# Feed-forward products of a two-layer retention kernel: split low-precision pairs replaced by plain fp32

## The reference, cut to what matters

```python
# 1. retention with decay mask, group norm, gate, output product (L0_attn_ref) on X
# 2. the feed-forward block that the change is about (L0_ffn_ref), D_IN = 256, D_HID = 1024
def _tlin(x, w, s): return jnp.einsum('bsi,oi->bso', x, w) * s
h = jax.nn.silu(_tlin(x, w1_w, w1_s)) * _tlin(x, w2_w, w2_s)
h = jax.nn.gelu(_tlin(h, h1_w, h1_s), approximate=False)
h = jax.nn.gelu(_tlin(h, h2_w, h2_s), approximate=False)
return _tlin(h, w3_w, w3_s)
# 3. a recurrence over a state of 32 blocks of 8 x 8, four steps (the batch axis) per position
# 4. a two-product mix with the previous position (L1_ffn_ref)
```

## Time and profile before

| | us |
|---|---|
| median of three runs | 1184.78 (1183.74 to 1186.15) |
| the profiled execution, its own time | 1184.52 |
| its span in the trace | 1182.7 |
| PE busy / DVE busy / ACT busy / POOL busy | 1083.8 / 965.1 / 606.7 / 483.6 |
| mean granted clock of TensorE | 0.968 of 2.4 GHz |

### The profile page before, as it was taken

The page is one execution under the profiler, slowest core; times in us unless marked ns, Lnnn a source line. Parts: engine busy times, 40 slices in busy tenths (PEclk is TensorE's granted clock), DMA queues, the critical chain, the costliest instruction groups (busy, mean ns, idle before and its releaser), DMA issues.

```text
span 1182.7 us, 16467 instructions
## 1 busy us (share of the span) xinstructions
PE 1083.8 (92%) x5761; PEld 837.7 (71%) x5761; DVE 965.1 (82%) x1417; ACT 606.7 (51%) x1039; POOL 483.6 (41%) x379
## 2 busy tenths in 40 slices
PE   6999999999999999999999999999999999984434
PEld 3666666677787777788778778877877887772323
DVE  3688888872045998998899899899989989999883
ACT  1345555554345356555735655573565557344552
POOL 1366677774333234344324433432343343231220
PEclk9999999999999999999999999999999999998657
DMA  6334544753522431332333133233313323310000
GB/s 227 128 138 159 190 174 176 275 189 110 175 90 72 134 97 52 110 111 85 95 101 126 44 115 101 94 91 98 130 40 120 96 82 90 95 48 0 0 18 21
DMA packets 45339, 127.02 MB, mean 107 GB/s; under 512 B 4320, under 2 KB 21472, under 8 KB 43104
## 3 DMA queue, kind: packets, MB, share of 16 engines
q1 hardware_dynamic: 44416, 114.72, 30.3%
q10 hardware_dynamic: 864, 11.54, 2.6%
HBM read 117.86 MB, written 19.92 MB: 117 GB/s over the span
## 4 chain that ended last, share of the span: by engine, by line
DVE 55%; PE 25%; issue 9%; ACT 6%; POOL 2%; DMA 1%; DVEq 0%; ACTq 0%; POOLq 0%; SPq 0%
DVE tmp L2015 7%; PE lower L441 7%; PE lower L1164 6%; DVE tmp L2005 6%; DVE Sq L2007 5%; DVE tmp L2021 4%; DVE delta L2017 4%; PE bank L1164 3%; DVE stats L142 2%; PE lower L541 2%; DVE delta L2019 2%; DVE S L2023 2%; ACT look L646 1%; DVE whole L1967 1%; PE bank L471 1%
## 5 line engine op out<-in xcount | busy, mean ns | idle before, releaser
L1830 POOL TENSOR_TENSOR a_lo<-whole,a_hi 128x512 fp32r<-128x512 f32 x128 | 181.8, 1438 | 268.3 <-ACT a_hi L1467 197.1
L1164 PE MATMUL lower<-b_hi,ring 128*128 128x512 f32 x512 | 193.6, 396 | 1.4 <-ACT a_hi L1467 1.4
L1164 PE MATMUL lower<-b_lo,ring 128*128 128x512 f32 x512 | 190.7, 390 | 1.7 <-POOL b_lo L1830 1.7
L1164 PE MATMUL lower<-a_hi,ring 128*128 128x512 f32 x496 | 186.3, 394 | 1.7 <-issue 1.7
L1164 PE MATMUL lower<-a_lo,ring 128*128 128x512 f32 x496 | 184.2, 390 | 0.2 <-POOL a_lo L1830 0.2
L1830 POOL TENSOR_TENSOR b_lo<-whole,b_hi 128x512 fp32r<-128x512 f32 x64 | 93.9, 1474 | 145.1 <-ACT b_hi L1467 145.1
L1450 ACT ACTIVATE S<-S 128x1024 f32<-128x1024 f32 x56 | 58.6, 1059 | 183.0 <-DVE S L2023 183.0
L1466 ACT ACTIVATE whole<-lower,hs 128x512 f32<-128x512 f32 x126 | 86.2, 684 | 76.8 <-PE lower L1164 71.8
L441 PE MATMUL lower<-wa,xT 128*128 128x512 f32 x240 | 111.2, 608 | 10.9 <-DMA wa<-wa_dram 8.0
L1164 PEld LDWEIGHTS lower<-b_hi,ring 128*128 128x128 f32 x512 | 96.2, 188 | 21.9 <-issue 1.8
L1164 PEld LDWEIGHTS lower<-b_lo,ring 128*128 128x128 f32 x512 | 96.0, 188 | 22.0 <-POOL b_lo L1830 2.3
(11 more groups left out here) (278 smaller groups left out, 2361.5 us busy)
## 6 DMA issues: line engine op xcount, KB each, us to landing
ring<-ffn_copy_dram SPq DMA_DIRECT2D x128, 512.0 KB, 3.6
look<-ffn_dram ACTq DMA_DIRECT2D x6, 1879.0 KB, 7.0
ffn_copy_dram<-ffn_dram SPq DMA_DIRECT2D x8, 1408.0 KB, 9.5
xT<-xT_dram SPq DMA_DIRECT2D x8, 512.0 KB, 8.5
rope<-rope_dram SPq DMA_DIRECT2D x8, 512.0 KB, 8.3
xtok<-x_dram SPq DMA_DIRECT2D x8, 512.0 KB, 4.4
x1in<-x_dram SPq DMA_DIRECT2D x8, 512.0 KB, 4.8
x1res<-x_dram SPq DMA_DIRECT2D x8, 512.0 KB, 3.3
```

Source lines behind the costliest of these rows:

```text
L1164: ins = nc.tensor.matmul(out, a, b, start=(first and n == 0), stop=(last and n == len(pairs) - 1))
L1830: nc.gpsimd.tensor_tensor(lo[:, m, :], t["whole"][:, m % 4, :], hi[:, m, :].bitcast(F32), ALU.subtract).then_inc(lo_done, 1)
```

## The change

The branch, the look at the weights and the copy in DRAM go. All feed-forward products are plain fp32 matmuls: the weight tiles and the moving tiles are of type fp32, and a block is one instruction in the program instead of two. The high and low tiles are gone, so all weights fit in SBUF: w1, w2, w3 as before, and `h1` and `h2` (4 MB each), loaded once in 16 pieces behind waits for the attention tiles whose place they take. The results of a layer alternate between an `inner` and a `middle` tile of six slots; two slots of each go to `pairs0` or `pairs1`, which change sides with the parity of the chunk, so the loop of bodies 3 to 6 becomes two rounds of two bodies. Activations write their tile once. The layout of some attention tiles changes with it. The GpSimd stream of a body has only the roots of the layer norms left.

```diff
-        w1r = sb(narrow, "w1r", [P, KD, HID], F32R)
-        w2r = sb(narrow, "w2r", [P, KD, HID], F32R)
-        w3r = sb(narrow, "w3r", [P, KH, DIM], F32R)
+        w1 = sb(top, "w1", [P, KD, HID])
+        w2 = sb(top, "w2", [P, KD, HID])
+        w3 = sb(top, "w3", [P, KH, DIM])
...
-            def copy_piece(c):
-                cols = bass.ds(c * PIECE, PIECE)
-                sp.dma_start(ffn_s[:, cols], ffn_d[:, cols]).then_inc(copy_in, 16)
...
-            def look_load(c):
-                act.dma_start(look[:], ffn_d[:, bass.ds(c * LOOK_STEP, LOOK)]).then_inc(look_in, 16)
-
-            def add_low_bits(c):
-                act.wait_ge(low_bits, c + 1)
-                nc.scalar.activation(look[:], look[:].bitcast(I32), ACT.Copy,
-                                     accum_out=low_sum[:, bass.ds(c, 1)]).then_inc(low_added, 1)
...
+            def first_side(m, parity):
+
+                return pairs[parity][:, m, :] if m < 2 else inner[:, m - 2, :]
+
+            def second_side(m, parity):
+
+                return middle[:, m, :] if m < KH - 2 else pairs[1 - parity][:, m - (KH - 2), :]
...
+            def schedule(eng, body):
+
+                for i in range(3):
+                    body(i, i % 2, True, i >= 1, i >= 2, i + 1 < CHUNKS)
+                with eng.Fori(3, CHUNKS - 2, 2) as i:
+                    body(i, 1, True, True, True, True)
+                    body(i + 1, 0, True, True, True, True)
+                body(CHUNKS - 1, 1, True, True, True, False)
...
+                    sp.wait_ge(proj_done, CHUNKS * BATCH)
+                    for m in (0, 3, 4):
+                        hidden_load(0, m)
+                    sp.wait_ge(rope_done, CHUNKS * BATCH)
+                    for m in (1, 2):
+                        hidden_load(0, m)
+                    sp.wait_ge(r1_done, (CHUNKS - 2) * 2)
+                    xtok_load(CHUNKS - 1, 1)
                     sp.wait_ge(yT_ps, (CHUNKS - 1) * 2)
+                    for m in (5, 6, 7):
+                        hidden_load(0, m)
+                    store(CHUNKS - 3, 1)
+                    sp.wait_ge(yT_ps, CHUNKS * 2)
+                    sp.wait_ge(gw_done, CHUNKS * 4)
+                    for m in range(KH - 1):
+                        hidden_load(1, m)
                     store(CHUNKS - 2, 0)
...
-                            if narrow_w:
-                                w = (w1r, w2r)[n]
-                                pairs = [(w[:, k, cols], x[:, k, :]) for k in range(KD) for x in (t["x1hi"], t["x1lo"])]
...
+                            ins = product(bank[pair(m, c) + n][:], [((w1, w2)[n][:, k, m * P:m * P + P], wide_a[:, k, :])
+                                                                    for k in range(KD)])
...
-                        ins = product(bank_of(n, c)[:], [(w[:, k, :], x[:, k, :]) for k in range(KH) for x in (hi, lo)])
+                        ins = product(bank_of(n, c)[:], [(w[:, m, k, :], src(k, parity))], first=(k == 0),
+                                      last=(k == KH - 1))
...
-                    act.wait_ge(lo_done, c * SPLITS + KH + n - 3)
-                    nc.scalar.activation(t["whole"][:, m % 4, :], bank_of(n, c)[:], ACT.Gelu, scale=scale).then_inc(act_done, 1)
-                    nc.scalar.activation((t["b_hi"], t["a_hi"])[layer][:, m, :], bank_of(n, c)[:], ACT.Gelu,
-                                         scale=scale).then_inc(hi_done, 1)
+                    nc.scalar.activation((second_side, first_side)[layer](m, parity), bank_of(n, c)[:], ACT.Gelu,
+                                         scale=(hs1, hs2)[layer][:, m:m + 1]).then_inc(act_done, 1)
...
-                pe.wait_ge(flag_done, 1)
+                    pe.wait_ge(turn_done, CHUNKS * BATCH)
+                    pe.wait_ge(v_done, CHUNKS * BATCH)
+                    pe.wait_ge(gate_done, CHUNKS * BATCH)
...
+                    act.wait_ge(r1_done, CHUNKS * 2 - 2)
                     silu(5)
```

More of the change, by code:

```diff
@@ L26 @@
 F32 = mybir.dt.float32
-F32R = mybir.dt.float32r
 I32 = mybir.dt.int32
@@ L136, in build @@
         w123_in = sem(top, "w123_in")
+        hidden_in = [[sem(top, f"hidden_in{n}_{m}") for m in range(KH)] for n in range(2)]
         pow_ready = sem(top, "pow_ready")
@@ L243, in build @@
             v[n] = sb(attention, f"v{n}", [P, BATCH, DIM])
-            xtok[n] = sb(attention, f"xtok{n}", [P, BATCH, DIM])
+            if not n:
+                xtok[n] = sb(attention, f"xtok{n}", [P, BATCH, DIM])
         state = sb(attention, "state", [P, BATCH, GROUPS, P])
@@ L1053, in fin_sums, with sync_program, hidden_load @@
                 return ((t["mv3"], t["mean3"]), (t["mv4"], t["mean4"]), (t["mv2"], t["mean2"]))
[L1055 to L1065, removed]
+            def schedule(eng, body):
[5 more added lines that the diff above has]
+                body(CHUNKS - 1, 1, True, True, True, False)
+            def sync_program(sp, store, xtok_load):
                 def x1_rows(c):
                     return x1_d[bass.ds(c, 1)].rearrange("o p b d -> (o p) b d")
[L1070 to L1075, removed]
+                def hidden_load(n, m):
+                    col = (COL_H1, COL_H2)[n] + m * HID
+                    sp.dma_start((h1, h2)[n][:, m].rearrange("p k n -> p (k n)"),
+                                 ffn_d[:, col:col + HID]).then_inc(hidden_in[n][m], 16)
                 out_view = out_d.rearrange("b (c p) d -> p c b d", p=P)
@@ L1125, in body @@
                                      t["y4"][:]).then_inc(out_done, 16)
-                    if more and narrow_w:
-                        for n in range(RING):
-                            ring_load(i + 1, n, i * 2 * KH + 2 * KH - RING + n + 1)
-                schedule(sp, body, 1 if narrow_w else 0)
+                schedule(sp, body)
                 for g, (c, n) in enumerate(PAIRS_LEFT):
@@ L1231, in down @@
-                def down(c):
-                    if narrow_w:
-                        pe.wait_ge(hi_done, c * SPLITS + 3 * KH)
-                        pe.wait_ge(lo_done, c * SPLITS + 3 * KH - 1)
-                    else:
-                        pe.wait_ge(act_done, c * 2 * KH + 2 * KH)
+                    w = (h1, h2)[layer]
+                    src = (first_side, second_side)[layer]
+                    if isinstance(c, int) and c == 0:
+                        pe.wait_ge(hidden_in[layer][m], 16)
@@ L1281, in mix_in, with body @@
                     by_row(wide_b, wr, 6, dr_ps)
-                def body(i, ffn, scan, mix, more):
+                def body(i, parity, ffn, scan, mix, more):
                     c, d = i - 1, i - 2
-                    started = narrow_w and isinstance(i, int) and i == 0
+                    started = isinstance(i, int) and i == 0
                     if ffn and not started:
@@ L2093, in ffn_out, with body @@
                     ln2.end()
-                def body(i, ffn, has_scan, mix, more):
+                def body(i, parity, ffn, has_scan, mix, more):
                     c, d = i - 1, i - 2
                     if has_scan:
-                        ffn_out(c, (lambda: product(i, 2)) if ffn else None)
-                    if ffn and not (narrow_w and isinstance(i, int) and i == 0):
+                        ffn_out(c, (lambda: product(i, parity, 2)) if ffn else None)
+                    if ffn and not (isinstance(i, int) and i == 0):
                         for m in range(3 if has_scan else 2, KH):
-                            product(i, m)
+                            product(i, parity, m)
                     if mix:
@@ L2114, in body @@
                         mix_result(d)
-                    if more and narrow_w:
-                        x1_low(i + 1)
                     if has_scan:
@@ L2330, in start @@
                     end.norm_stats(last, 1)
-                if narrow_w:
-                    start()
-                    prepare()
-                else:
-                    prepare()
-                    for m in range(2):
-                        product(0, m)
+                start()
+                prepare()
                 schedule(dve, body)
@@ L2419, in _ @@
             def _(dve):
-                end = attention_vector(dve)
-                flag = wide_words(dve)
-                with dve.If(flag < 1):
-                    steps = vector_program(dve, True, end)
-                with dve.Else():
-                    attention_ends(dve, end.body)
-                    assert vector_program(dve, False, end).k == steps.k
+                steps = vector_program(dve, attention_vector(dve))
                 last_mix(dve, steps)
```

419 lines of the change are left out of this document (98 added, 321 removed).

## The result

| | before | after |
|---|---|---|
| median of the runs | 1185.3 us (1183.74 to 1186.15, 4 runs) | 1728.39 us (1727.13 to 1732.06, 4 runs) |
| profiled execution, its span | 1184.52, 1182.7 us | 1728.57, 1726.6 us |
| ratio of the runs, 95% interval | | 1.4589 (1.4562 to 1.4617) |

A forecast was written before the change was run, and what follows sets the result against it. TensorE was taken as the bound, so its added work is paid nearly in full: 1184.5 + 517 + 48.6 - 8.6 - 4.5 - 2.4 = 1734.6, forecast 1735 us, range 1700 to 1790.

The forecast's parts named there:

- The bound: Feed-forward pipeline: TensorE idles only 9.6 of 822 us, so added work is paid nearly in full; period 103.7 to 174.4 us.
- The price of a wide block: `up` and `hidden`, 512 columns: 0.8575 us in plain fp32 against 0.4537 as a split pair; 1280 blocks, +517 us.
- The three checks that the forecast set: Bodies: period near 174 us with PE busy throughout, DVE below 60%; `hidden` blocks starting 0.857 us apart, two records each.
- The price of a narrow block: `down`, 256 columns: 0.43 us in plain fp32 against 0.24 a split pair; 256 blocks, +48.6 us (43 to 50).
- Products, gaps and `down` together: Feed-forward pipeline: +517 us for `up` and `hidden`, +48.6 for `down`, -8.6 of PE's 9.6 us idle time.
- The look and the attention stage: Attention stage: removing ScalarE's six 3.355 us looks at the weights and DVE's masks gives -4.5 us, bounds 0 and -7.9.
- The loads of h1 and h2, the waits added, the longer loop: Weight loads, new waits, two-body loop: 0 us; late pieces 3 us each, 24 at most; loop up to 2 a round.
- Is PE fed: Top of a body, x2 transposes: PE runs 17.2 us of `up` after `down` instead of 9.1; slack grows from 1 to 9.
- The end: After the last `down`: first key norm 3.4 us after row 0's turn instead of 5.8, -2.4 us; remaining 115.4 us stay.
- Two passes: Rival, feed-forward products: an fp32 product costs one record's step, 0.429 us instead of 0.4537, giving 1131 us; chance 0.04.
- PE starved once a body: Rival, bodies: tanh waits behind Gelus, VectorE's scan delivers late; 10 us in each of 7 bodies, 1805 us; chance 0.09.
- The clock: Rival, feed-forward products: denser fp32 work lowers the clock; a tenth at 1.2 GHz adds 120 us, 1855 us; chance 0.03.

## Why the prediction was right

- **The bound.** Right. TensorE had no slack, and the whole price of its work showed: the period forecast as 174.4 us is 174.4.
- **The price of a wide block.** Right. Read off four blocks of `mix_in`, it holds in `hidden` (0.859), and the period of 174.4 us says that it holds for the rest. The three checks that the forecast set are met: period, step of 0.859, two records to a product.
- **The price of a narrow block.** 0.432 measured against 0.43.
- **Products, gaps and `down` together.** +517 + 48.6 - 8.6 = 557 forecast, 554.1 between the marks in the trace: 3 us too much. The price in isolation is 562 to 564 us, against 565.6; PE's busy time between the marks rose by 563.4 (813.5 to 1376.9). Why that is 2 us under eight times the difference of the periods (70.7) was not followed. The gaps went almost altogether, some 9.5 and not 8.6 us.
- **The look and the attention stage.** -4.5 forecast. -5.7 in the trace of the changed kernel, -5.9 with the look taken out of the kernel before, inside the bounds of 0 and -7.9. The cause was right; the size was a choice between the bounds, and off by a little over 1 us.
- **The loads of h1 and h2, the waits added, the longer loop.** At nothing, rightly: from 235 to 1610 us there is no PE gap for any of them. But their place in the queue is not free of charge: where an experiment put copies in front and s3 was issued 10 us later, TensorE waited 7 to 11 us and lost some clock.
- **Is PE fed.** After the last record of `down` at 919.9 the transposes of x2 start at 937.1 us, 17.2 us later, as forecast; nothing waits.
- **The end.** The step that was mis-sized most for its size: -2.4 forecast, -4.5 measured. The part that was worked out holds: from row 0's turn at 1609.93 to the first key norm at 1613.27 it is 3.3 us (forecast 3.4). The part held constant, 115.4 us, did not stay. The rows are the windows from that norm to the last instruction, before and after:

```profile
1067.30:1182.70 115.40, 45.84 (x144) 32.68 (x142) 83.73 (x153) 51.98 (x123) 22.30 (x25) 0.67 0.03 10
```

```profile
1613.27:1726.60 113.33, 44.33 (x144) 31.51 (x142) 83.71 (x153) 51.87 (x123) 21.67 (x25) 0.71 0.03 10
```

The same instructions, VectorE's busy time the same to 0.02 us; PE's clock is 0.71 instead of 0.67 in it and its work 1.5 us shorter. That goes with the 2.1 us; that it is their cause was not tried.

**The rivals.** Two passes: refuted by the period and by the step, and by the two kernels with the same copies in which nothing but the kind of product differs (1174 and 1738 us). The Trainium skill, "FP8 and Floating Point Precision", TensorE Precision Notes, counts four passes for true fp32; the step of 0.859 is 3.8 of the fp32r steps of 0.2268, near it. Half the rate, which the Trainium skill's "Perfetto Trace Analysis", Engine Utilization, gives for FP32_LOW_HIGH, is near what one of the two records takes (0.429 us, 1.9 fp32r steps), but not the product: against an fp32r matmul that is a little over a quarter, and the measurement decides. That the name stands for one record is not shown. PE starved once a body: refuted, there is no gap in 1375 us. The clock: 1.00 from 235 to 1610 us.

All misses have one sign: the sum of 1734.6 lay 6.0 us above the profiled execution's 1728.6; the terms were 2.9 us too high in the products and gaps, 1.2 in the attention stage and 2.1 at the end (6.2 together, since they are counted in the spans).

## What to carry to other kernels

Before a trick is taken out because it doubles the instructions, price one block with and without it by the steps from start to start, in the trace at hand: two fp32r matmuls (0.454 us) were cheaper than one fp32 product (0.859), though the page counts two records for both. Where the same engine is busy for a whole period, that difference times the number of blocks was here the answer to a per cent, and whatever the other engines and the DMA queues were relieved of was worth only the gaps that the bound had (all of that came to some 20 us, beside 563). The one load that cost anything here was the last ahead of the point where a stage waits for all of its constants: issued 10 us later, it cost 9.4 us.

## What of the hardware was not expected

- A stall costs more than its length. A wait of TensorE of 6.8 us near 232 us was followed by a granted clock of 0.50 up to 242.5 us (a mean of 0.93 from 240 to 260), and the execution was 8.3 us longer. With 20% of gaps in the bodies the mean clock was 0.90, without gaps 1.00. Not every gap does it: in the attention stage, with 4% of gaps, it was 1.00 too.
- Two-input VectorE operations of 128x1024 had been longer in the kernel before, at the same shape. The groups of the kernel before and of the one after, all in the recurrence (count, busy us, mean ns, idle):

```profile
L2015 DVE TENSOR_TENSOR tmp<-S,kvq 128x1024 f32<-128x1024 f32 x42 | 81.3, 1937 | 1.4
```

```profile
L1803 DVE TENSOR_TENSOR tmp<-S,kvq 128x1024 f32<-128x1024 f32 x42 | 51.4, 1225 | 1.4
```

  and with the helpers' idle work put back into the changed kernel, another line of the same loop (1225 ns without it):

```profile
L1838 DVE TENSOR_TENSOR S<-S,tmp 128x1024 f32<-128x1024 f32 x42 | 55.3, 1316 | 1.4
```

  The look had no part in it (1939 ns without it, the ring and the helpers kept), and the traffic put back lengthened VectorE's period by nothing (83.75 us). GpSimd's work put back lengthened it by 1.6 us (84.00 to 85.56).

  The mean of 1937 ns hides two lengths. Of the 42 records of line 2015, 12 took 1.22 or 1.23 us and 30 took more, all but one of them 2.15 to 2.27. At the start of each of the 30 a subtraction of GpSimd (line 1830) was under way; at the start of the 12 none was, or one that ended within 0.04 us. From both engines' timelines:

```profile
640.07 1.29 POOL L1830 TENSOR_TENSOR a_lo<-whole,a_hi 128x512 fp32r<-128x512 f32 x1 [3.41 <-ACT a_hi L1467]
640.17 2.27 DVE L2015 TENSOR_TENSOR tmp<-S,kvq 128x1024 f32<-128x1024 f32 x1
...
606.49 1.23 DVE L2015 TENSOR_TENSOR tmp<-S,kvq 128x1024 f32<-128x1024 f32 x1
```

  The long record ends 1.08 us after GpSimd's does (642.44 and 641.36), as if VectorE had begun only then; the record at 382.96 us, with 0.61 us of the subtraction left, took 1.69. The reductions of the same loop, with one input (line 2007 before, 1795 after), took 1220 ns in both kernels. Line 2015 is hit most because in this schedule it often starts 0.1 us behind a subtraction. With the idle subtractions put back only 4 of the 42 records of line 1838 met one, at 2.18 us each: that is why so little of the slowness came back.
